# Handing the feed-forward's inner tile over in chunks of 128 channels, in a fused two-layer kernel

## The reference, cut to what matters

```
x = x + L0_conv(ln_c(x));  t = tokens(x);  x = image(t + L0_ffn(ln_t(t)))
x = x + L1_conv(ln_c(x));  t = tokens(x);  x = image(t + L1_ffn(ln_t(t)))

def ffn(x, W1, b1, W2, b2):          # 96 -> 384 -> 96
    h = relu(qlinear(x, W1, b1))
    return qlinear(h, W2, b2)
def qlinear(x, W, b):                # q_mul: 5 exponent, 2 mantissa bits; q_acc: 5 and 10
    y = q_acc(einsum('bsk,nk->bsn', q_mul(x), q_mul(W)))
    return q_acc(y + q_mul(b))
```

## Time and profile before

| | |
|---|---|
| time of 3 runs | median 8133.32 us (8124.04 to 8137.58) |
| profiled execution | 8123.94 us, its span 8122.1 us |
| TensorE granted clock, mean | 0.865 |
| busy share of the span | PE 76%, DVE 68%, ACT 58%, POOL 7% |
| instructions L744, L751, L880 | 512, 512 and 1536 |

### The profile page before, as it was taken

The page is one execution under the profiler, slowest core; times in us unless marked ns, Lnnn a source line. Parts: engine busy times, 40 slices in busy tenths (PEclk is TensorE's granted clock), DMA queues, the critical chain, the costliest instruction groups (busy, mean ns, idle before and its releaser), DMA issues.

```text
span 8122.1 us, 110800 instructions
## 1 busy us (share of the span) xinstructions
PE 6148.7 (76%) x40192; PEld 2370.1 (29%) x40192; DVE 5512.9 (68%) x9325; ACT 4740.2 (58%) x7907; POOL 568.9 (7%) x366
## 2 busy tenths in 40 slices
PE   2777778778778778778778777777787787787775
PEld 1223223333223333223233233332233332232221
DVE  5666777666776666776667776667766667766664
ACT  1455665655656556656556656556565566565555
POOL 0000000000000000000000000000000000000000
PEclk8888888888889888888888898888898888898887
DMA  1222322323322323322223223223223233232222
GB/s 40 51 70 65 82 72 60 76 62 73 82 64 64 77 63 76 81 54 72 71 67 80 74 60 75 64 70 84 68 60 77 62 75 81 54 72 72 64 65 61
DMA packets 395480, 556.40 MB, mean 69 GB/s; under 512 B 71491, under 2 KB 391428, under 8 KB 391772
## 3 DMA queue, kind: packets, MB, share of 16 engines
q1 hardware_dynamic: 394940, 549.32, 27.8%
HBM read 233.66 MB, written 78.68 MB: 38 GB/s over the span
## 4 chain that ended last, share of the span: by engine, by line
PE 41%; DVE 29%; ACT 11%; DMA 9%; issue 7%; SPq 3%; POOL 0%; DVEq 0%; ACTq 0%; POOLq 0%
DVE conv L828 14%; PE bank L552 9%; PE bank L526 5%; PE bank L567 5%; PE b_banks L632 4%; PE bank L505 4%; DMA r_b<-rstd_row_c 4%; PE bank L554 3%; PE b_banks L651 2%; DMA r_b<-rstd_row_b 2%; ACT L779 2%; PE bank L642 2%; PE b_banks L587 2%; DMA r_a<-rstd_row_a 2%; DVE hidden L880 1%
## 5 line engine op out<-in xcount | busy, mean ns | idle before, releaser
L828 DVE SCALAR_TENSOR_TENSOR conv<-mid,w_dw,conv 128x1568 f32<-128x1568 f32 x1536 | 2830.6, 1843 | 14.1
L505 PE MATMUL bank<-xc_a,w_exp 128*128 128x392 f32 x1536 | 827.1, 638 | 463.3 <-DVE xc_a L811 423.4
L967 POOL TENSOR_TENSOR x<-x,xc_a 96x392 f32<-96x392 f32 x256 | 551.3, 2153 | 7042.4 <-DVE xc_a L811 7042.4
L587 PE MATMUL b_banks<-xn,w_q 128*128 128x392 fp8e5 x1536 | 390.1, 368 | 714.1 <-DVE xn L872 672.5
L632 PE MATMUL b_banks<-shifted,w_combo 128*32 128x392 f32 x6144 | 748.3, 540 | 31.8 <-DMA shifted<-g 31.0
L552 PE MATMUL bank<-conv,w_proj_gated 128*96 128x392 f32 x2048 | 760.2, 516 | 0.0
L744 ACT ACTIVATE hidden<-b_banks 128x1176 f16<-128x1176 f32 x512 | 589.9, 1152 | 208.8 <-PE b_banks L587 207.3
L851 DVE SCALAR_TENSOR_TENSOR x<-bank,bn_bias,r_a 96x392 f32<-96x392 f32 x256 | 159.2, 622 | 812.0 <-PE bank L554 812.0
L567 PE MATMUL bank<-x,centering 128*96 128x392 f32 x1536 | 653.4, 517 | 61.7 <-ACT sq_b L663 43.3
L751 ACT ACTIVATE hidden<-hidden 128x1176 fp8e5<-128x1176 f16 x512 | 608.1, 1188 | 33.7 <-DVE hidden L880 30.9
L662 ACT ACTIVATE g<-bank 96x392 f32<-96x392 f32 x512 | 252.5, 493 | 589.2 <-PE bank L567 320.9
(11 more groups left out here) (158 smaller groups left out, 8718.6 us busy)
## 6 DMA issues: line engine op xcount, KB each, us to landing
phases_on<-phases SPq DMA_DIRECT2D x768, 101.5 KB, 2.2
shifted<-g SPq DMA_DIRECT2D x512, 149.6 KB, 2.8
r_b<-rstd_row_b SPq DMA_DIRECT2D x512, 147.0 KB, 2.9
shifted<-g SPq DMA_DIRECT2D x256, 199.5 KB, 2.9
x<-in_x SPq DMA_DIRECT2D x32, 1176.0 KB, 7.8
r_a<-rstd_row_a SPq DMA_DIRECT2D x256, 147.0 KB, 3.4
x_plus_norm<-x SPq DMA_DIRECT2D x256, 147.0 KB, 2.1
r_a<-x_plus_norm SPq DMA_DIRECT2D x256, 147.0 KB, 2.2
```

The costliest lines, as they stand in the source:

```text
L505: mm(ring[bank][:, 0:TW], WEXP[:, 128 * k:128 * k + 128], xc_tile(t, 128), start=True, stop=True)\
L587: last = mm(PB[:, c, 0:TW], W1Q[:, f, 128 * c:128 * c + 128], XN8[t % 2][:, :], start=True, stop=True)
L828: v.scalar_tensor_tensor(out=acc, in0=src, scalar=WDW[:, k, j:j + 1], in1=acc, op0=ALU.mult, op1=ALU.add).then_inc(sem["convolved"], 1)
L967: g.tensor_tensor(tile(XA, t), tile(XA, t), xc_tile(t), ALU.add).then_inc(sem["xplus_a"], 1)
```

## The change

The inner tile is handed over in three parts at each step. PE signals `up_done` after each of its 3 matmuls and waits for `up_evacuated` chunk by chunk; ACT's one eviction of 128x1176 becomes 3 of 128x392, each with its wait and signal; DVE's 3 bias instructions each wait for their own chunk and signal `biased`; ACT's one conversion becomes 3; PE's down matmuls each wait for their own chunk of `quantised`. The counts of these semaphores run three times as fast, and other waits on them (norm, conv1) are scaled. Order of steps, buffers and due times stay.

```
 PE, up
-                pe.wait_ge(sem["up_evacuated"], at(NT * (2 * m + f) + t))
+                before = NHC * (NT * (2 * m + f) + t)
                 pe.wait_ge(sem["normed_b"], at(NT * (3 * m + 2 * f) + t + 1))
                 for c in range(NHC):
-                    last = mm(PB[:, c, 0:TW], W1Q[...], XN8[t % 2][:, :], start=True, stop=True)
-                last.then_inc(sem["up_done"], 1)
+                    pe.wait_ge(sem["up_evacuated"], at(before - NHC + c + 1))
+                    mm(PB[:, c, 0:TW], W1Q[...], XN8[t % 2][:, :], start=True, stop=True)
+                        .then_inc(sem["up_done"], 1)
 PE, down
-                pe.wait_ge(sem["quantised"], at(NT * (2 * m + f) + t + 1))
                 for c in range(NHC):
+                    pe.wait_ge(sem["quantised"], at(NHC * (NT * (2 * m + f) + t) + c + 1))
                     last = mm(ring[bank][0:C, 0:TW], W2Q[:, f, c, :], Q8[t % 2][:, c, :], ...)
 PE, conv1, first tile
-                    pe.wait_ge(sem["up_evacuated"], at(NT * (2 * b + 1)))
+                    pe.wait_ge(sem["up_evacuated"], at(NHC * NT * (2 * b + 1)))
 ACT, up
-                act.wait_ge(sem["quantised"], at(q - 1))
-                act.wait_ge(sem["up_done"], at(q + 1))
-                f(Y16[t % 2][:, :, :], PB[:, 0:NHC, 0:TW], ACT.Copy).then_inc(sem["up_evacuated"], 1)
+                act.wait_ge(sem["quantised"], at(NHC * (q - 1)))
+                for c in range(NHC):
+                    act.wait_ge(sem["up_done"], at(NHC * q + c + 1))
+                    f(Y16[t % 2][:, c, :], PB[:, c, 0:TW], ACT.Copy).then_inc(sem["up_evacuated"], 1)
 ACT, quant
-                act.wait_ge(sem["biased"], at(q + 1))
-                f(Q8[t % 2][:, :, :], Y16[t % 2][:, :, :], ACT.Copy, saturate=False)
-                    .then_inc(sem["quantised"], 1)
+                for c in range(NHC):
+                    act.wait_ge(sem["biased"], at(NHC * q + c + 1))
+                    f(Q8[t % 2][:, c, :], Y16[t % 2][:, c, :], ACT.Copy, saturate=False)
+                        .then_inc(sem["quantised"], 1)
 DVE, norm
-                    dve.wait_ge(sem["up_done"], at(NT * (2 * m + L // 2) + t - 1))
+                    dve.wait_ge(sem["up_done"], at(NHC * (NT * (2 * m + L // 2) + t - 1)))
 DVE, quant
-                dve.wait_ge(sem["up_evacuated"], at(q + 1))
                 for c in range(NHC):
-                    last = v.tensor_scalar(Y16[t % 2][:, c, :], ..., ALU.add, ALU.max)
-                last.then_inc(sem["biased"], 1)
+                    dve.wait_ge(sem["up_evacuated"], at(NHC * q + c + 1))
+                    v.tensor_scalar(Y16[t % 2][:, c, :], ..., ALU.add, ALU.max)
+                        .then_inc(sem["biased"], 1)
```

More of the change, by code:

```diff
@@ L583, in tensor_steps @@
                 m = e if f else b
-                pe.wait_ge(sem["up_evacuated"], at(NT * (2 * m + f) + t))
+                before = NHC * (NT * (2 * m + f) + t)
                 pe.wait_ge(sem["normed_b"], at(NT * (3 * m + 2 * f) + t + 1))
                 for c in range(NHC):
-                    last = mm(PB[:, c, 0:TW], W1Q[:, f, 128 * c:128 * c + 128], XN8[t % 2][:, :],
-                              start=True, stop=True)
-                last.then_inc(sem["up_done"], 1)
+                    pe.wait_ge(sem["up_evacuated"], at(before - NHC + c + 1))
+                    mm(PB[:, c, 0:TW], W1Q[:, f, 128 * c:128 * c + 128], XN8[t % 2][:, :],
+                       start=True, stop=True).then_inc(sem["up_done"], 1)
             elif name == "down":
@@ L749, in scalar_steps @@
                 act.wait_ge(sem["down_done"], at(q - 1))
-                act.wait_ge(sem["biased"], at(q + 1))
-                f(Q8[t % 2][:, :, :], Y16[t % 2][:, :, :], ACT.Copy, saturate=False)\
-                    .then_inc(sem["quantised"], 1)
+                for c in range(NHC):
+                    act.wait_ge(sem["biased"], at(NHC * q + c + 1))
+                    f(Q8[t % 2][:, c, :], Y16[t % 2][:, c, :], ACT.Copy, saturate=False)\
+                        .then_inc(sem["quantised"], 1)
             elif name == "down":
@@ L876, in vector_steps @@
                 q = NT * (2 * (e if g else b) + g) + t
-                dve.wait_ge(sem["up_evacuated"], at(q + 1))
                 for c in range(NHC):
-                    last = v.tensor_scalar(Y16[t % 2][:, c, :], Y16[t % 2][:, c, :], B1Q[:, g, c:c + 1], 0.0,
-                                           ALU.add, ALU.max)
-                last.then_inc(sem["biased"], 1)
+                    dve.wait_ge(sem["up_evacuated"], at(NHC * q + c + 1))
+                    v.tensor_scalar(Y16[t % 2][:, c, :], Y16[t % 2][:, c, :], B1Q[:, g, c:c + 1], 0.0,
+                                    ALU.add, ALU.max).then_inc(sem["biased"], 1)
             elif name == "add":
```

## The result

The changed kernel takes 8214.44 us (median of 4 runs, 8212.3 to 8220.69) against 8128.68 us before (4 runs, 8122.2 to 8137.58): ratio 1.0106, 95% interval 1.0089 to 1.0124. It is 86 us slower; the forecast was 49 us slower. The profiled execution took 8214.22 us, its span 8212.4 us.

What follows compares the result with a forecast made beforehand. No engine was near 100%: a kernel of stages with separate limits, ACT nearly saturated in the FFN stretches. 0.77 us in each FFN over 32 images gave +49 on 8133, so 8182 us, own range 8150 to 8215.

Steps and rivals of the forecast that it cites:

- Price per tile: ACT's split instructions: eviction +0.10 us and conversion +0.19 us a tile, 148 us if all were on the path.
- The bound by a fixed part as small as PSUM's: ACT's conversion: lower bound of +0.10 us a tile if its fixed part equals the PSUM copy's; +0.19 was taken.
- PE's and DVE's waits and signals at nothing: Added waits and signals on DVE's bias and PE's matmuls: taken as 0, with 0.2 us per tile kept for PE.
- How much is on the path: ACT's 0.29 us per tile in FFN 1 and FFN 0: 0.77 us of each stage reaches the path.
- The sum: Both FFN stages over all images: (0.77 + 0.77) x 32 = +49 us.
- Nothing is late behind that which has a reserve: Stretch behind the FFN stages, DVE's Newton steps and a DMA round trip: just starts later, no further cost.
- what would make it wrong: Changed DVE or PE instructions further apart, TensorE's clock falling where it is 1.00, or up running early enough to advance ACT's work.
- PE pays for the waits: Rival: waits on PE's matmuls hold back weight loads, 0.2 us per tile, half on the path; 8234 us, chance 0.07.
- The faster rival: Shorter handoffs eviction to bias and bias to conversion win 29 us if ACT's extra is absorbed; 8104 us, chance 0.18.
- Its condition: Faster rival decides if ACT's lateness at FFN 1's last conversion is under 0.46 to 0.47 us; worked out as 1.05.
- What the trace should show: Evictions 0.38 us apart, conversions 0.42 to 0.43, ACT busy up 150 us or more, shorter waits, pass 247.7 us.

Runs made afterwards that it cites:

- the filled kernels: Small constant matmuls added where PE idles: changed kernel, 20 in FFN 1 and 16 in FFN 0, 8174.89 us; kernel before, 16 in FFN 0, 8123.23 us.
- FFN 1 filled: Changed kernel with the small constant matmuls in PE's idle time in the back of FFN 1 only: 8188.63 us, ratio 1.0079 to the kernel before.

## Why the prediction came out as it did
- **Price per tile:** right. Forecast 0.10 and 0.19 us, measured 0.10 and 0.18. The bound by a fixed part as small as PSUM's (+0.10 for the conversion) is refuted: two more SBUF copies cost 0.09 us each. This also agrees with the 93 ns for SBUF of the Trainium skill (Perfetto Trace Analysis, Optimizing Scalar/DVE Operations).
- **PE's and DVE's waits and signals at nothing:** right, by the kernel with ScalarE whole (0.9991).
- **How much is on the path:** the working gave 0.77 us for each stage; passes with a full clock show 0.83 and 0.82, and with the clock held up in the FFN stages of both kernels the difference is 52 us (48 against the plain kernel before), against the forecast's 49. Per stage the filled kernels show 0.69 and 0.64, which is 43 us in 32 passes; the remainder stands in the rest of the pass, where the forecast had nothing, so a part of the agreement is luck.
- **The sum, +49 for 86 measured:** the step that failed is "Nothing is late behind that which has a reserve". PE was: behind its longer wait in FFN 1 it works at the lower clock, a cost for which the sum has no term and which the forecast only listed under what would make it wrong. By the filled kernels the clock is 34 to 38 us of the 86, some 25 of it in FFN 1. The trace before held the warning: in FFN 0 the clock fell in 5 of 30 passes, and in the back of FFN 1 PE already stood idle for 1.28 us at full clock.
- **"PE pays for the waits"** went in the right direction by the wrong mechanism: PE pays for being left without work, not for the waits as instructions.
- **The faster rival:** of the chain's two handoffs the eviction's does shorten, and by itself it is worth 0.2 to 0.3%; the 0.47 us gap at the bias was used up by ACT's lateness. Its condition, ACT less than about 0.47 us late at the last conversion of FFN 1, fails with both splits and holds with the eviction alone (4 x 0.10 = 0.4). That it decides at this point fits the measurements, but was only argued; no run varied the lateness alone.
- **What the trace should show:** distances 0.38 and 0.42, the smaller waits and the gap before the last conversion gone (4084.19 to 4084.61 is the distance of adjacent instructions): all there. ACT's busy time rose by 129 us where I asked for 150 or more; the distances give 0.28 x 512 = 143, and why 14 of them don't show is open. The pass grew by 3.1 us, not by 1.5.

Open: why only some passes lose the clock. In the changed kernel 7 of 30 keep it in FFN 1 with the same last wait of PE; no run here separates what differs in them. Open too: how much of the loss in FFN 0 the change brings about. Its 16 passes (15 with FFN 1 filled) stand against 5 before, but the kernels that only move signals or split the eviction lose 2 to 8 there, those with the conversion split 7 and 14, the one with both split and whole handoffs 11, and the wait behind which it happens is for a row load. The numbers by pass come from one execution of each kernel.

## What to carry to other kernels
Before cutting an instruction up for an earlier handoff, look whether its engine is the saturated one in that stretch: the fixed part is paid each time there (0.05 us from PSUM, 0.09 from SBUF on ScalarE), and an earlier signal wins only where its receiver stands waiting. Cut the one whose cut is cheap and whose handoff is waited for: here the eviction (DVE waited 69.7 us for it, ACT 30.9 for the biases). And when a change makes one engine late, ask how long TensorE is now without work and what its clock is in the stretches behind: here the change cost some 50 us directly and another 34 to 38 that came back when TensorE was kept busy.

## What was unexpected of the hardware
- A few tenths of a us more idle time of TensorE (1.58 instead of 1.28 us, after shorter gaps) went with a fall from the upper to the lower clock level in 23 of 30 passes, and constant-only matmuls in the gaps kept it up in 30 of 30. The length of the wait alone doesn't decide: the 7 passes that kept the clock had the same one, and with 1.40 and 1.47 us it was lost in 0 and 6 of 30 (2 in the other kernel with 1.47).
- The listed duration of an ACT instruction grows in an unbroken run while its distance to the next doesn't: the same activation of 128x392 is listed with 0.50 us in the kernel before and with 0.61 in the changed kernel, each 0.37 to 0.38 before the next. Durations in a saturated stretch are no price; distances are.
